# One transposing product for four shift rows: a softmax shift carried by twelve rows of ones

## The reference

```
q, k, v = proj(layernorm(x), Wq, bq), proj(ctx, Wk, bk), proj(ctx, Wv, bv)   # 16 heads of 16
scores = einsum('bhqd,bhkd->bhqk', q, k) / sqrt(16)
attn = softmax(scores, axis=-1)                                               # over 1601 keys
x = x + einsum('bhqk,bhkd->bhqd', attn, v) @ Wo.T + bo
```

## Time and profile before

| | |
|---|---|
| time, median of 3 runs | 701.7 us (701.22 to 702.26) |
| the profiled execution | span 699.7 us; the page gives no other time of it |
| TensorE busy | 671.0 us, 96% |
| TensorE weight loads busy | 507.2 us, 72% |
| VectorE busy | 552.5 us, 79% |
| ScalarE busy | 443.4 us, 63% |
| GpSimd busy | 549.0 us, 78% |

### The profile page before, as it was taken

The page is one execution under the profiler, slowest core; times in us unless marked ns, Lnnn a source line. Parts: engine busy times, 40 slices in busy tenths (PEclk is TensorE's granted clock), DMA queues, the critical chain, the costliest instruction groups (busy, mean ns, idle before and its releaser), DMA issues.

```text
span 699.7 us, 21737 instructions
## 1 busy us (share of the span) xinstructions
PE 671.0 (96%) x8632; PEld 507.2 (72%) x8681; DVE 552.5 (79%) x1138; ACT 443.4 (63%) x885; POOL 549.0 (78%) x374
## 2 busy tenths in 40 slices
PE   4799999999999999999999999999999998899897
PEld 2556786877777877787778777877777786677673
DVE  4697877868888878778787868787868788888867
ACT  2446766666666666676767666767675787665830
POOL 7759999999699889798989789889788786723422
PEclk9999999999999999999999999999999999999999
DMA  8587055454445454545353645363543450000212
GB/s 309 143 213 214 27 138 162 99 155 97 150 113 155 105 164 92 160 107 165 93 165 84 178 102 159 85 187 89 169 97 104 100 164 4 2 2 9 91 69 91
DMA packets 45610, 84.20 MB, mean 120 GB/s; under 512 B 8668, under 2 KB 28420, under 8 KB 45508
## 3 DMA queue, kind: packets, MB, share of 16 engines
q1 hardware_dynamic: 43896, 80.13, 41.9%
q0 software_dynamic: 912, 2.14, 1.0%
q10 hardware_dynamic: 704, 0.55, 0.3%
HBM read 36.89 MB, written 6.55 MB: 62 GB/s over the span
## 4 chain that ended last, share of the span: by engine, by line
PE 82%; DVE 5%; DMA 5%; SPq 2%; issue 2%; POOL 2%; ACT 2%; ACTq 0%; DVEq 0%; POOLq 0%
PE ps_kv L821 17%; PE ps_kv L812 16%; PE ps_score L872 12%; PE ps_out L896 12%; PE ps_front L844 12%; PE ps_score L920 2%; SPq L502 2%; DMA kstack<-khigh 2%; PE ps_out L912 1%; DMA cbuf<-in_ctxT 1%; PE ps_kv L783 1%; DMA wq_sb<-in_wqT 1%; PE ps_front L920 1%; PE ps_front L853 1%; PE ps_kv L920 1%
## 5 line engine op out<-in xcount | busy, mean ns | idle before, releaser
L637 POOL TENSOR_TENSOR plow<-prob 128x1024 bf16<-128x1024 f32 (+1 forms) x198 | 372.1, 1898 | 58.8 <-ACT prob L1242 56.3
L1511 DVE TENSOR_REDUCE maxes<-ps_front 128x1 f32<-128x512 f32 (+1 forms) x416 | 267.1, 666 | 57.2 <-PE ps_front L844 53.9
L1242 ACT ACTIVATE prob<-ps_score 128x512 f32<-128x512 f32 (+1 forms) x416 | 236.2, 598 | 71.0 <-PE ps_score L872 61.9
L872 PE MATMUL ps_score<-qstack,kstack 98*128 98x128 bf16 (+1 forms) x1664 | 150.5, 219 | 0.8 <-ACT prob L1242 0.5
L844 PE MATMUL ps_front<-kstack,qstack 96*128 96x512 bf16 (+1 forms) x512 | 145.4, 333 | 2.7 <-DMA kstack<-khigh 1.9
L872 PEld LDWEIGHTS ps_score<-qstack,kstack 98*128 98x128 bf16 (+1 forms) x1664 | 112.1, 98 | 33.7 <-ACT prob L1242 1.9
L896 PE MATMUL ps_out<-vstack,prob 128*128 128x65 bf16 (+1 forms) x1664 | 113.6, 194 | 0.7 <-POOL plow L637 0.3
L821 PE MATMUL ps_kv<-w_hi,cbuf 128*128 128x256 bf16 (+1 forms) x402 | 109.7, 273 | 0.9 <-DVE vstack L1501 0.9
L1494 DVE SCALAR_TENSOR_TENSOR klow<-ps_kv,bcol,khigh 128x512 bf16<-128x512 f32 (+1 forms) x123 | 76.8, 629 | 42.5 <-ACT khigh L1220 42.0
L821 PE MATMUL ps_kv<-w_hi,clow 128*128 128x256 bf16 (+1 forms) x402 | 109.5, 272 | 0.0
L821 PE MATMUL ps_kv<-w_lo,cbuf 128*128 128x256 bf16 (+1 forms) x402 | 109.5, 272 | 0.0
(11 more groups left out here) (290 smaller groups left out, 858.7 us busy)
## 6 DMA issues: line engine op xcount, KB each, us to landing
kstack<-khigh SPq DMA_DIRECT2D x256, 100.1 KB, 2.2
cbuf<-in_ctxT SPq DMA_DIRECT2D x15, 1601.0 KB, 7.2
kstack<-klow SPq DMA_DIRECT2D x128, 100.1 KB, 2.2
qstack<-q_blocks SPq DMA_DIRECT2D x48, 64.0 KB, 2.3
q_blocks<-qbd SPq DMA_DIRECT2D x16, 128.0 KB, 2.0
cbuf<-in_weT SPq DMA_DIRECT2D x2, 1024.0 KB, 7.8
slot_x<-att_all SPq DMA_DIRECT2D x8, 128.0 KB, 7.1
vstack<-slot_x SPq DMA_DIRECT2D x4, 256.0 KB, 3.6
```

The source lines that it names most:

```text
L637: nc.gpsimd.tensor_tensor(plow[slot][0:n, :], prob[slot][0:n, :], p_high(slot, 0, HP * P)[0:n], ALU.subtract).then_inc(plow_gps, 1)
L872: mm = nc.tensor.matmul(ps_score[0:nn, h % NSB, j * P:(j + 1) * P], kstack[par][0:98, hp, n0:n0 + nn], qstack[par][0:98, q_at(hp), :], sta ...
L1242: nc.scalar.activation(prob[slot][0:nn, e * 512:e * 512 + 512], ps_score[0:nn, h % NSB, :], ACT.Exp)\
L1511: nc.vector.reduce_max(maxes[:, hp:hp + len(unit), n], ps[:, 0:len(unit) * nn].rearrange("p (h k) -> p h k", k=nn), AX.X).then_inc(m_free, 1)
```

## The change

A half's four pairs are transposed by one product: mparts is now a slice of mwords with all twelve words of the half, behind 96 leading columns (zeros; in the second half the last twelve of them are the first half's words, whose rows are not read), so that twelve rows come out on partitions 96 to 107 for 128 columns (queries). spread_shift on VectorE then multiplies these twelve rows, repeated four times, by a mask that leaves to each pair its own two rows of shift parts and zeros the rest, and writes the 12 x 512 results into qstack. The keys have twelve rows of ones, and a score product contracts 108 rows. The copy on ScalarE and its letter R are gone; VectorE's string has 32 letters s, each a few places behind the maximum that ends a half; all else in the four strings, TensorE's and GpSimd's whole strings among it, is as before. The ones are loaded inside keys() of batches 0 and 1, after their key pieces. The mask is one addition of two slices of the identity.

```diff
+SHIFT_TOP = 96 + 3 * 4
...
-        mparts = [mwords[:, 3 * hp + 1:3 * hp + 99].bitcast(bf16)[:, 1::2] for hp in range(HP)]
+        mparts = [mwords[:, 12 * half:12 * half + SHIFT_TOP].bitcast(bf16)[:, 1::2] for half in range(2)]
+        shift_mask = sb("shift_mask", [P, 4])
...
-            sp.dma_start(kstack[0][96:98, :, :].rearrange("p a n -> p (a n)").bitcast(f32), ones2).then_inc(ld_ones, 16)
-            sp.dma_start(kstack[1][96:98, :, :].rearrange("p a n -> p (a n)").bitcast(f32), ones2).then_inc(ld_ones2, 16)
+            def load_ones(par):
+                sp.dma_start(kstack[par][96:SHIFT_TOP, :, :].rearrange("p a n -> p (a n)").bitcast(f32),
+                             ones2[0].partition_broadcast(SHIFT_TOP - 96)).then_inc((ld_ones, ld_ones2)[par], 16)
...
+                if b < 2:
+                    load_ones(par)
                 if b % 2 == 0 and b < B - 2:
                     send_queries(b // 2 + 1)
...
-                for j in range(4):
-                    mm = nc.tensor.matmul(ps_front[0:98, SHIFT_POS[half] % 2, j * P:(j + 1) * P],
-                                          mparts[4 * half + j], ident_bf[:, :], start=True, stop=True)
-                mm.then_inc(shift_done, 1)
+                nc.tensor.matmul(ps_front[0:SHIFT_TOP, SHIFT_POS[half] % 2, 0:P], mparts[half], ident_bf[:, :],
+                                 start=True, stop=True).then_inc(shift_done, 1)
...
-                                          kstack[par][0:98, hp, n0:n0 + nn], qstack[par][0:98, q_at(hp), :],
+                                          kstack[par][0:SHIFT_TOP, hp, n0:n0 + nn], qstack[par][0:SHIFT_TOP, q_at(hp), :],
...
-            def copy_shift(b, half):
-                act.wait_ge(shift_done, 2 * b + half + 1)
-                nc.scalar.copy(qstack[b % 2][96:98, half::2, :],
-                               ps_front[96:98, SHIFT_POS[half] % 2, :].rearrange("p (h c) -> p h c", h=4))\
-                    .then_inc(shift_copied, 1)
...
+                nc.vector.tensor_tensor(shift_mask[96:SHIFT_TOP, :], ident[96:SHIFT_TOP, 97:SHIFT_TOP:3],
+                                        ident[96:SHIFT_TOP, 98:SHIFT_TOP:3], ALU.add).then_inc(fills_set, 1)
...
+            def spread_shift(b, half):
+                dve.wait_ge(shift_done, 2 * b + half + 1)
+                if b == 0 and half == 0:
+                    dve.wait_ge(fills_set, 4)
+                nc.vector.tensor_tensor(qstack[b % 2][96:SHIFT_TOP, half::2, :],
+                                        ps_front[96:SHIFT_TOP, SHIFT_POS[half] % 2, 0:P].unsqueeze(1).to_broadcast([12, 4, P]),
+                                        shift_mask[96:SHIFT_TOP, :].unsqueeze(2).to_broadcast([12, 4, P]), ALU.mult)\
+                    .then_inc(shift_copied, 1)
```

More of the change, by code:

```diff
@@ L129 @@
 ACT_PROGRAM = [
[L130 to L138 removed]
+    ("KKgKKKKKKKKKKKKKKgKKKKKKKKKKKKKKeKeeeeKeKeeKeeKeeeeeeKKeeeeeeKeeeeKeeeKeKeeKeeKeeKeKeeKeKeeeegeKeKee"
+     "eKeKKeeKKeeeeKeeKeeKeKeeeKeeeKeeKeeKeeeKKeeKeKeKKeeeKeKeeeKeKeeKKeeeKeKeeKeeKeeeegeeKeKeKKKeeKeeKeKe"
+     "eKeeeeKeKeeKeeeKeeKeeKeeeKKeeKKKeKeeKeKeeKeeKeKKeKeeKeeeeeKKeeegeKeKeeeKeKKeKeeeKeeeKeKeeeKeeKeeKKee"
+     "eKeKeeKeKeKeeKKeKeKeeeKeeKeKeeeKeKeeKeeKeeKeKeegeKeeKeeKeKKeeKeeKeeKeKeeeKeeeKeKeeKeKeKeeKeKeeeKeeKK"
+     "eKeeKeeeKeeeKeKeeKeeKeeKeeKKeeKeegeKKeeKKeKeKeeeKKeeKeeeeeKeKeKeKeKeeeKKeeKeeeKeKeeKKeeKeeKeeKeeeeeK"
+     "eeKKeeKeKeKKeeegeKeeKeKKeKeeKeeKeeKeeKeeKeeeKeeKeeKeKeeKeeeKKeeKKeKeKeeeKeKeeeKKeeeeKeeeeKeKKeeeKeeK"
+     "eKeKeKKeKeeKeeeKeeKeeKeeKeKeeeKeKeeeeeZKeeeKeeeeeeAeeeeeAeeeeeeeeeeeeeHeeeHeeBATVTBVEEPPHEEVA2PTPBAH"
+     "2EEPfPHViBTV2ABTEEfPPifEEPi2PAHlAV2HBTffHiTiBElVEVPTPBEEPP2EE2PPxhfixylhfxyixl2yyfhil", 1),
@@ L139 @@
 ]
 DVE_PROGRAM = [
-    ("jKKKkKBzKkzKKCKmmmmmkmKmmjmmKmKmmKmKzmmKmKmmKmKmmKKmmKmKmKmKmmKmmmKmKmmmmKmKmmmmmKmmKmmmmmKmmKvKmmKm"
-     "mkmKmmKmmmmKmKmmmKmjmmKKmmKmmammKmKKmKKmmmKvmKmmmmKKmmmmKmmKmmmmKmKmKmmKmmmKmKKaKmmKmmKvmmKmKmmKmzKm"
-     "KmmmmKmammkjmmKmmKmKmmKmKKKvKKmmKmmmKmmmKKmmmKmmmmKmammKmmKmKmmKmmKmKKvKKmKmmmKmmKmmKzkmmaKmmmKmmKmK"
-     "mjmmKmKmmmKmmKmKKKvmKmamKmKmmmmmKKmmmKmKmmmmKmKmKmmmKmmKmKKmKKmmKmvKmKmmmKmmzmmmKmKmmKmmjKmmKmKammmK"
-     "mmKmKKKmKvmKmmKmmmmKmKkmmmKmKmammKmKmmKmmKmmmmKmKKKvmmKmmKmKmmKzmmmKamKmmmKmmKmmKjmmKKmmmKmmKmKKKKvm"
-     "KmmmKmmmKKmmmKmmKmmKmmmmKKmmmKmmmaKmKKmKKmmvmmKKmmmmKmKmaKmmmKmmKmKmjmmKmKmmmKmmKmKKKKvmKmamKmmmmKmm"
-     "KmmKmmmKmmmKmKmmKmmmKmKmKKmKmKmKmvmKmmmKKmmmmmaKmmKmKmmmKmKmKmmmKKmmKmKmKmmKvmmKmmKmKmmmmKmmmKmmmmmm"
-     "KmKmmmKmaZpvppppXDXGDNpGLpNTLppTpXDGMMUUNaMMULUWvTXDxGWdNMgMLUUnXDGTNxLadgWTnMMUxUdXgDMnMUGUWN1xL3WX"
-     "DdGTNgXDLGxdngNTnMMLU1UT3MMUUWMMUUWxdgnxdqg1nqWq31qxd3gnyyyy1yyffy3fyyffyyy", 1),
+    ("jKKKkKBzKkzKKCKmmmmmkmKmmjmmKmKmmKmKzmmKmKmmKmKmmKKmmKmsKmKsmKmmKmmmKmKmmmmKmKmmmmmKmmKmmmmmKmsmsKvK"
+     "mmKmmkmKmmKmmmmKmKmmmKmjmmKKmmKmmammKmKKsmsKKmmmKvmKmmmmKKmmmmKmmKmmmmKmKmKmmKmmmsKmKKsaKmmKmmKvmmKm"
+     "KmmKmzKmKmmmmKmammkjmmKmmKmKmmKsmKsKKvKKmmKmmmKmmmKKmmmKmmmmKmammKmmKmKmmKmmKsmKKsvKKmKmmmKmmKmmKzkm"
+     "maKmmmKmmKmKmjmmKmKmmmKmmKsmKKsKvmKmamKmKmmmmmKKmmmKmKmmmmKmKmKmmmKmmKmKKsmsKKmmKmvKmKmmmKmmzmmmKmKm"
+     "mKmmjKmmKmKammmKmmKsmKKsKmKvmKmmKmmmmKmKkmmmKmKmammKmKmmKmmKmmmmKsmKKsKvmmKmmKmKmmKzmmmKamKmmmKmmKmm"
+     "KjmmKKmmmKmmKsmKKsKKvmKmmmKmmmKKmmmKmmKmmKmmmmKKmmmKmmmaKmKsKmsKKmmvmmKKmmmmKmKmaKmmmKmmKmKmjmmKmKmm"
+     "mKmmKsmKKsKKvmKmamKmmmmKmmKmmKmmmKmmmKmKmmKmmmKmKmKsKmsKmKmKmvmKmmmKKmmmmmaKmmKmKmmmKmKmKmmmKKmmKsmK"
+     "smKmmKvmmKmmKmKmmmmKmmmKmmmmmmKmKmmmKsmaZspvppppXDXGDNpGLpNTLppTpXDGMMUUNaMMULUWvTXDxGWdNMgMLUUnXDGT"
+     "NxLadgWTnMMUxUdXgDMnMUGUWN1xL3WXDdGTNgXDLGxdngNTnMMLU1UT3MMUUWMMUUWxdgnxdqg1nqWq31qxd3gnyyyy1yyffy3f"
+     "yyffyyy", 1),
@@ L1326, in _ @@
             halves = iter([(b, h) for b in BATCHES for h in range(2 * NCH)])
-            shifts = iter([(b, half) for b in BATCHES for half in range(2)])
             query_tiles = iter(range(TILES))
@@ L1345, in _ @@
                     exponentials(*next(halves))
-                if letter == "R":
-                    copy_shift(*next(shifts))
                 if letter == "Z":
@@ L1725, in _ @@
             queries = {kind: iter(range(kind != "j", TILES)) for kind in "kzj"}
+            shifts = iter([(b, half) for b in BATCHES for half in range(2)])
             maxima = iter([(b, m) for b in BATCHES for m in range(MUNITS)])
@@ L1733, in _ @@
             for letter in program(DVE_PROGRAM):
+                if letter == "s":
+                    spread_shift(*next(shifts))
                 if letter == "q":
```

9 lines of the change are left out of this document (removed).

## The result

The kernel after the change takes 711.07 us (median of 4 runs, 710.87 to 712.51) beside 701.82 us (701.22 to 702.26) before it on the same chip: a ratio of 1.0138, 95% interval 1.0126 to 1.0150. It is 9.3 us slower. 698.6 was forecast, and 711.07 lies outside the range given.

What follows compares the result with a forecast made beforehand. TensorE was taken as the bound from about 90 to 570 us; -5.3 + 0.3 (batch 0's halves) + 1.4 (VectorE) + 0.5 (keys) + 0 (start) = -3.1, giving 698.6 us, range 695.4 to 701.7.

Steps and rivals of the forecast that it cites:

- TensorE, 32 x 0.165 us: Transposing products on TensorE: one in place of four saves 0.165 us in each of 32 halves, 5.3 us.
- Rows at no cost, ScalarE's copies nothing: Score products contracting 108 rows in place of 98 cost zero; removing ScalarE's 32 copies, 18.5 us, gives nothing of its own.
- A multiply occupies 0.60 us.: VectorE: each added multiply lasts 0.68 us, less 0.08 of overlap, so occupies 0.60; 19 us in all.
- An idle gap absorbed it: VectorE's idle gaps absorb most multiply pushes; TensorE loses 1.4 us in all, batch 10 being tightest in the steady part.
- Keys, 0.5 us: Where TensorE already waits for the next batch's keys, time saved only lengthens the wait: three batches cost 0.5 us.
- I take 0, near the middle: Moved loads of ones: earlier start against delay of batch 2's context, -0.9 to +1.2 us, taken as 0.
- Both prices worked out there: Hold-up of batch 2's context by the ones: 2.1 us for one row per engine, 1.6 spread over all sixteen.
- the first: Rival: TensorE waits for VectorE's multiply at first halves' ends, +4.3 us, 706.0 us; chance 0.08.
- the second: Rival: ones collide with batch 2's context in full and the start gains nothing, +2.0, 700.6 us; chance 0.15.
- both signs that the prediction gives for it: Signs of ones delaying batch 2's context: GpSimd's context wait ends past 53 us, TensorE waits over 2 us at 64.
- Rival 3: Saving hidden: GpSimd paces the kernel or TensorE isn't as full as its starts say; 701.7 us, no change; chance 0.10.

Runs made afterwards that it cites:

- four_products: Kernel after the change with three more copies of its one product in each half, multiply and ones kept: 710.92 us, ratio 1.0113 to the kernel before.
- multiply_alone: Kernel before with VectorE's 32 multiplies added, 432 columns on partitions 64 to 75, result unused: 706.24 us, ratio 1.0067.
- ones_alone: Kernel before with twelve rows of ones in place of two, loaded behind the first two batches' key pieces: 705.72 us, ratio 1.0068.
- multiply_low: Kernel before with VectorE's 32 multiplies added, 432 columns on partitions 0 to 11, result unused: 704.99 us, ratio 1.0052.
- masked_keys: Kernel after the change without its multiply: mask in the keys' ones, one ScalarE copy a half, ones loaded at other times: 702.15 us, ratio 1.0007 to before.
- after_phase: Kernel after the change with 80 one-column matmuls (160 instructions) ahead of TensorE's program: 709.41 us, ratio 1.0091 to the kernel before.
- masked_phase: masked_keys with 80 one-column matmuls ahead of TensorE's program: 699.95 us, ratio 0.9966 to the kernel before.
- masked_counted_wide: masked_counted with its fillers taking the product's own weights in 96 columns in place of one: 700.97 us, ratio 0.9972 to the kernel before.
- masked_counted: masked_keys with three one-column matmuls behind each of its 32 products, restoring the old instruction count: 704.04 us, ratio 1.0037 to the kernel before.

## Why the prediction was wrong

Taken alone, the ones cost 4.8 us and the multiply 4.7, together 9.5 us, about the 9.3 that the change costs; and the 5.3 us of removed products, which should stand against them, came to nothing (four_products). The sum had 0 for the ones, 1.4 for the multiply and 0.5 for keys. That the two single costs add up so well is in part luck: multiply_alone has a shorter multiply, and ones_alone keeps the packets in place. Step by step:

- **TensorE, 32 x 0.165 us.** The pitch was right: a shift's difference to before falls by 0.16 to 0.17 us in every half whose product is not waited for. That this is worth the same in time was wrong, for two reasons below.
- **Rows at no cost, ScalarE's copies nothing.** Right: 65-column and 128-column scores keep their pace (219 ns), and no wait of before was the copies'.
- **"A multiply occupies 0.60 us."** This term was mis-sized. The duration was right (0.696 to 0.698 us against 0.68), but it pushes what follows by 0.80 us in batch 10, since it overlaps neither neighbour. The estimate took an overlap of 0.08 us from rows in which all instructions begin at partition 0 (the line that it quotes gives 0.04; 0.08 is what most neighbours have); the multiply begins at 96. The Trainium skill has the rule, which the prediction did not weigh: "VectorE: DVE Perf Modes", section "Two Vector instructions with no wait between them", says that an instruction whose input or output begins in another group of 32 partitions than the last one's starts only when all earlier ones have finished. multiply_alone and multiply_low agree with it (+0.03 against -0.07 to -0.09 us).
- **"An idle gap absorbed it", 1.4 us.** This step failed. Batch 10 was forecast to wait 0.40 us at its second product and waits 0.65. But the places counted were mostly the second products (five waits, 1.4 us), and the larger sum is at the key projections (nine waits, 3.2 us, of which one of 0.2 us was there before): the low part of keys behind a multiply frees its bank late. The prediction named these low parts and took the slack before them for enough. The last multiply of batch 15, with TensorE's next score right behind it, costs 1.02 us more. multiply_alone measures 4.7 us where TensorE is not early and no score waits for the multiply, over three times the sum's 1.4.
- **Keys, 0.5 us.** Mis-sized, and for a cause that the sum did not have: 3.1 us of waits, 2.7 of them in batches 9 and 10, behind instruction packets that the smaller program moved. masked_keys has them without the multiply, after_phase, masked_phase, masked_counted_wide and four_products have none in that stretch.
- **The ones, "I take 0, near the middle" of -0.9 to +1.2.** The start came as forecast (first maxima at 27.47 us against 27.7, the query sends landed by 18.9). The hold-up was 2.9 us on the context against bounds of 0 to 2.1, the query sends were held up as well, and the clock fell behind TensorE's wait (1.62 us), which no step had. Of the rule of the Trainium skill that the prediction cites ("DMA: Bandwidth & Descriptors", section "Why a DMA increments its semaphore by 16 and not by 1"), twelve engines with one row each, the trace shows twelve packets that move at the same time, which fits; no row shows which engine moves which. Both prices worked out there, 2.1 and 1.6 us, were too low.

Of the rivals, the first came nearest in kind and in time (706.0), though at another place, and the second was true as well: both signs that the prediction gives for it, GpSimd past 53 us and TensorE waiting over 2 us at 64, are in the profile. The prediction treated them as alternatives and priced each from the rows of an undisturbed kernel. Rival 3 was right in its first half, that the saving is hidden, but not through GpSimd.

What stays open: masked_phase and masked_counted_wide gain 2.4 and 2.0 us where the pitch alone would give up to 5.3, and not all of the difference is placed; how much of the change's 9.3 us the clock took in each run, and of the 4.8 us of ones_alone; what lengthens some executions outside the span by 0.7 us; and why a packet on the instruction queue holds the sync queue's issue.

## What to carry to other kernels

Work saved on a full engine is worth its size only if the transfers and the engines that feed it have as much room; before adding an instruction to an engine at 80%, take its push from neighbours that begin at the same partition as it will. A change in the number of instructions also moves their fetches against the loads, by microseconds here: before judging such a change by its time, look whether the loads that are needed first have been hit, and time it again with the packets moved by idle instructions, which may as well move the loss (after_phase) as take it away (masked_phase). Put a small-looking load of few, long rows where no larger one is waited for next.

## What the runs showed of the hardware

- Of the key pieces issued in the half microsecond after a 16 KB packet of the instruction queue began to move (0.9 to 1.6 us each), 22 of 24 in the kernel before took 0.9 to 1.9 us to issue in place of 0.6. They land after 3.2 us (median) in place of 2.2, and pieces in flight are late too, up to 4.0 us after the change. That such a block is 256 instructions is also what the Trainium skill states, "Advanced Engine Details and Errata", section "ISA Cache"; here 70 packets stand against 17.9 thousand instructions of TensorE.
- A VectorE instruction on partitions that begin at 64 or 96 between two that begin at 0 costs some 0.11 us at each border (0.08 us of overlap lost, 0.03 us of gap): 1.41 us against 1.18 in multiply_alone and multiply_low.
- A matmul with one column of weights behind one with 108 started 0.15 us after it (masked_counted), one with 96 columns from the same tile 0.055 us (masked_counted_wide).
- A row of 25.6 KB moved as one packet and took 2.3 to 3.1 us ahead of batch 2's context. Twelve of them ahead of a context of 1601 KB made this one 2.9 us longer.
